# GpSimd's first level of the sums over negated scores: two heads in one instruction

## The reference, cut to what matters

```python
h = relu(layernorm(x))
q, k, v = h @ Wq.T, h @ Wk.T, h @ Wv.T + bv          # split into 12 heads
scores = q @ k.T * 384 ** -0.5 + bias                # 256 x 256 for each head; bias is 2 adj, then adj
row_nonzero = any(scores != 0, axis=-1)
p = softmax(where(row_nonzero, scores, -inf))        # nan becomes 0
x = x + (p @ v) @ Wo.T + bo
```

## Time and profile before

| what | value |
|---|---|
| median of 3 runs | 1733.27 us (1732.4 to 1737.6) |
| profiled execution, its own time | 1735.73 us |
| span of the profile | 1733.9 us |
| granted TensorE clock, mean | 0.994 |
| PE busy | 1661.9 us (96%) |
| DVE busy | 1545.5 us (89%) |
| ACT busy | 1356.5 us (78%) |
| POOL busy | 1360.2 us (78%), 1801 instructions |

### The profile page before, as it was taken

The page is one execution under the profiler, slowest core; times in us unless marked ns, Lnnn a source line. Parts: engine busy times, 40 slices in busy tenths (PEclk is TensorE's granted clock), DMA queues, the critical chain, the costliest instruction groups (busy, mean ns, idle before and its releaser), DMA issues.

```text
span 1733.9 us, 46852 instructions
## 1 busy us (share of the span) xinstructions
PE 1661.9 (96%) x14208; PEld 1496.1 (86%) x14208; DVE 1545.5 (89%) x5126; ACT 1356.5 (78%) x4233; POOL 1360.2 (78%) x1801
## 2 busy tenths in 40 slices
PE   6999999999999999999999999999999999999997
PEld 5888888888988888888889889888888888898885
DVE  6999999988989989889899899899999998998985
ACT  5878788788777787877887877787878878778775
POOL 4788787887877887878878878878778788788785
PEclk9999999999999999999999999999999999999998
DMA  7535535546446455355464464453553544544532
GB/s 228 122 85 127 121 95 137 112 100 141 101 111 139 91 123 125 94 134 113 99 141 105 107 141 94 118 131 93 130 121 93 138 109 104 141 94 118 132 72 67
DMA packets 92089, 201.50 MB, mean 116 GB/s; under 512 B 14528, under 2 KB 50880, under 8 KB 91840
## 3 DMA queue, kind: packets, MB, share of 16 engines
q1 hardware_dynamic: 91840, 198.50, 48.8%
HBM read 34.87 MB, written 12.58 MB: 27 GB/s over the span
## 4 chain that ended last, share of the span: by engine, by line
PE 93%; DVE 4%; issue 1%; POOL 1%; DMA 0%; ACT 0%; DVEq 0%; SPq 0%; POOLq 0%; ACTq 0%
PE misc_bank L735 23%; PE probT_bank L690 19%; PE misc_bank L775 13%; PE score_bank L672 11%; PE misc_bank L754 11%; PE values_bank L707 11%; PE values_bank L763 3%; PE misc_bank L715 2%; DVE values L532 2%; DVE normed L509 2%; ACT prob L410 0%; DMA stack<-split_qk 0%; DMA rows<-x 0%; DVE neg L548 0%; POOL quarter L336 0%
## 5 line engine op out<-in xcount | busy, mean ns | idle before, releaser
L410 ACT ACTIVATE prob<-neg,neg_max 128x256 f32<-128x256 f32 x1536 | 764.5, 501 | 124.9 <-DVE neg_max L548 110.5
L548 DVE CUSTOM_DVE_ANT_0 neg<-score_bank,bias 128x256 f32<-128x256 f32 x1536 | 577.7, 419 | 138.8 <-PE score_bank L672 124.5
L331 POOL TENSOR_TENSOR half<-neg 128x256 f32<-128x256 f32 x768 | 552.1, 737 | 163.1 <-DVE neg_max L548 162.8
L690 PE MATMUL probT_bank<-identity,prob 128*128 128x128 f32 x3072 | 430.6, 272 | 3.6 <-ACT prob L410 1.8
L421 ACT ACTIVATE probT<-probT_bank 128x512 f32<-128x512 f32 x640 | 368.2, 586 | 54.7 <-PE probT_bank L690 36.1
L690 PEld LDWEIGHTS probT_bank<-identity,prob 128*128 128x128 f32 x3072 | 353.2, 141 | 7.4 <-ACT prob L410 4.1
L672 PE MATMUL score_bank<-stack 96*128 96x256 f32 x1536 | 344.1, 313 | 2.6 <-DMA stack<-split_qk 2.1
L410 ACT ACTIVATION_READ_ACCUMULATOR prob<-neg,neg_max 128x1 f32 x1536 | 290.7, 189 | 0.0
L336 POOL TENSOR_TENSOR quarter<-half 128x512 f32<-128x512 f32 x192 | 248.0, 1292 | 15.1
L672 PEld LDWEIGHTS score_bank<-stack 96*128 96x128 f32 x1536 | 233.1, 191 | 29.2 <-issue 26.2
L707 PE MATMUL values_bank<-probT,values 128*32 128x256 f32 x3072 | 205.6, 385 | 1.1 <-ACT probT L421 1.1
(11 more groups left out here) (93 smaller groups left out, 3961.7 us busy)
## 6 DMA issues: line engine op xcount, KB each, us to landing
stack<-split_qk SPq DMA_DIRECT2D x768, 192.0 KB, 4.1
bias<-adj SPq DMA_DIRECT2D x64, 256.0 KB, 4.0
rows<-x SPq DMA_DIRECT2D x30, 384.0 KB, 4.5
out<-rows SPq DMA_DIRECT2D x30, 384.0 KB, 4.7
own_rows<-x SPq DMA_DIRECT2D x2, 384.0 KB, 4.7
out<-own_rows SPq DMA_DIRECT2D x2, 384.0 KB, 3.6
neg<-w0q SPq DMA_DIRECT2D x1, 576.0 KB, 4.4
prob<-w0k SPq DMA_DIRECT2D x1, 576.0 KB, 5.6
```

Of the source, the lines that this page charges most:

```text
L331: nc.gpsimd.tensor_tensor(half[:, step % GROUP, :, :], n[:, :, 0:N // 2], n[:, :, N // 2:N], ALU.add).then_inc(half_done, 1)
L410: nc.scalar.activation(prob[:, step % PROB, q, :], neg[:, step % NEG, q, :], ACT.Exp, scale=-1.0, bias=neg_max[u.k % 2][:, step, q:q + 1], ...
L548: nc.vector.tensor_tensor_reduce(out=neg[:, step % NEG, q, :], in0=score_bank[step % 2][:, q * N:(q + 1) * N], in1=bias[u.k % 4][:, q, :], ...
L690: mm = nc.tensor.transpose(probT_bank[step % 2][:, k * N + q * P:k * N + (q + 1) * P], prob[:, step % PROB, q, k * P:(k + 1) * P], identit ...
```

## The change

`add_half` takes two heads: it waits until both are negated, adds the halves of both in one instruction, and counts two. GpSimd's list is written anew for the pairs: six `add_half` for a unit in place of twelve. The half of head 0 no longer stands at the end of the slot before, but goes with head 1 at the start of its unit's own slot; `split_heads` of group 0 follows the first pair; `add_output_bias` stands ahead of the pair of heads 8 and 9. Nothing on the other engines is changed, their waits included.

```diff
@@ -326,10 +326,10 @@
             def add_half(u, step):
 
-                pool.wait_ge(neg_done, u.count(2 * HEADS, 2 * step + 2))
-                n = neg[:, step % NEG, :, :]
-                nc.gpsimd.tensor_tensor(half[:, step % GROUP, :, :], n[:, :, 0:N // 2], n[:, :, N // 2:N], ALU.add
-                                        ).then_inc(half_done, 1)
+                pool.wait_ge(neg_done, u.count(2 * HEADS, 2 * step + 4))
+                n = neg[:, step % NEG:step % NEG + 2, :, :].rearrange("p a q k -> p (a q) k")
+                h = half[:, step % GROUP:step % GROUP + 2, :, :].rearrange("p a q k -> p (a q) k")
+                nc.gpsimd.tensor_tensor(h, n[:, :, 0:N // 2], n[:, :, N // 2:N], ALU.add).then_inc(half_done, 2)
 
@@ -378,12 +378,11 @@
             def slot(attend, project, output, norm):
                 for stage, u, i in (
-                    (add_half, attend, 1), (add_half, attend, 2), (split_heads, output, 0), (add_half, attend, 3),
+                    (add_half, attend, 0), (split_heads, output, 0), (add_half, attend, 2),
                     (add_rest, attend, 0), (split_heads, output, 1), (split_heads, output, 2),
-                    (add_half, attend, 4), (add_half, attend, 5), (add_half, attend, 6), (add_half, attend, 7),
-                    (add_rest, attend, 1), (add_half, attend, 8), (add_output_bias, project, 0),
-                    (add_half, attend, 9), (invert_deviation, norm, 0), (add_half, attend, 10),
-                    (add_half, attend, 11), (add_rest, attend, 2), (add_half, project, 0),
+                    (add_half, attend, 4), (add_half, attend, 6),
+                    (add_rest, attend, 1), (add_output_bias, project, 0), (add_half, attend, 8),
+                    (invert_deviation, norm, 0), (add_half, attend, 10), (add_rest, attend, 2),
                 ):
```

## The result

The changed kernel takes 1777.38 us (median of 4 runs, 1775.57 to 1778.02), the kernel before beside it 1732.84 us: a ratio of 1.025, 95% interval 1.023 to 1.027. It is slower, as forecast, by 44.5 us where 25 were forecast; the time lies in the range. Between the two profiled executions the difference is 1775.57 - 1735.73 = 39.8 us.

The account below looks back on a forecast made before the run. A slot loop of PE and VectorE legs, with VectorE stretched by GpSimd's port use, was taken as the bound; 0.40 us over 61 slots plus 0.6 gave +25 us, median 1758, range 1734 to 1788.

Parts of the forecast that it names:

- What bounds the kernel: Each slot loops through PE (transposes to head 8's scores) and VectorE (head 8 to second value bias): 26.46 us.
- what the saved GpSimd work is worth: 73 us less work on GpSimd, worth nothing on the path because GpSimd has idle time.
- The price of a pair: One two-head `add_half` on GpSimd takes 1.28 us, like `quarter`; two single halves take 1.47.
- the spacing rule: Time GpSimd by start-to-start spacing: `quarter` at most 1.39 us; used for a pair, 40 us more, 1798.
- The end of the slot: Pair of heads 10 and 11 waits for head 11, delaying `quarter` and the normalisations: 0.43 us a slot.
- The sum: 0.40 us a slot over 61 slots, 24.4, plus 0.6 for the program's ends: +25 us, median 1758.
- The first half of the slot and group 1: From the first pair to `shares` of group 1: head 8 0 to 0.1 us late, group 0's `shares` 0.05.
- the slower turn: At `nonzero` of group 1, some slots before already had the delay: about 0.03 us a slot taken off.
- The range: The forecast time lies between 1734 and 1788 us, with about 0.80 of the chance.
- The bounds: Up to six pair prices a slot: 0.03 less each gives -11 us, 0.05 more each +18 us.
- two halves in disguise: GpSimd's pair takes the time of two halves, 1.47 us, giving 1825 us; chance 0.07.
- The first rival: At the slot's end the second normalisation gets the port before `quarter`, 1.08 us earlier: 1694 us; chance 0.11.

Follow-up runs that it names:

- the run with this pair alone: The kernel before with only heads 10 and 11 joined into one pair instruction, all other halves single: 1760.70 us, ratio 1.015.
- the first kernel with the added wait: The changed kernel, with GpSimd waiting for both normalisations after the pair of heads 10 and 11, before `quarter` of group 2: 1716.19 us, ratio 0.989.
- the kernel before with the added wait: The kernel before, with GpSimd waiting until both normalisations are done ahead of `quarter` of group 2: 1679.62 us, ratio 0.968.

## Why the prediction was right, and where its size was off

*What bounds the kernel* was right: two legs, PE and VectorE, and the loss on VectorE's. So was what the saved GpSimd work is worth: nothing.

*The price of a pair*, 1.28, measured 1.285. In the prediction the spacing rule of the Trainium skill (Perfetto Trace Analysis, "GPSIMD Engine Instruction") was applied across a semaphore and gave 1.39. This trace has two pairs in a row, and their starts, 907.32 and 908.58, are 1.26 apart, so that rule and the printed span nearly agree; across a semaphore it is 1.36 (919.13 to 920.49). And the VectorE instruction that stood behind the pair at 914.23 ended by its printed span: `nonzero` at 914.51 + 1.03 = 915.54, 0.02 after 914.23 + 1.29. Of the 73 us of work that GpSimd was to be spared, the line of the halves shows 60.7 (552.1 - 491.4), since busy time counts the overlap of two halves in a row once, and `eighth` takes 4.8 more. The second of the two pairs in a row, in a narrower window of GpSimd's timeline:

```profile
908.58 1.29 POOL L332 TENSOR_TENSOR half<-neg 128x512 f32<-128x512 f32 x1
```

*The end of the slot* was right in mechanism and near in size. The sum had 0.33 us there (0.43 less the 0.10 from earlier in the slot); the run with this pair alone shows 0.39, the two normalisations taking 2.62 in place of 2.23, and that is the 24.5 us between the profiled executions. The difference of 0.06 is the hop: I had 0.09 us from the negation to the pair, taken from single halves, and it was 0.15, since an increment of two puts the wait into an instruction of its own. That is a cost of the diff that I did not read out of it; undone in all pairs it is worth 8.5 us.

*The first half of the slot and group 1* is the other mis-sized term. I had head 8 at most 0.1 us late and head 11 0.10 late; head 8 was 0.15 late and head 11 0.22. Count from the value bias that opens the slot. These lines are of the kernel before, and then of the changed one, the last of them GpSimd's:

```profile
874.43 0.54 DVE L532 TENSOR_TENSOR values<-misc_bank,v_bias 128x384 f32<-128x384 f32 x1
...
877.76 0.42 DVE L548 CUSTOM_DVE_ANT_0 neg<-score_bank,bias 128x256 f32<-128x256 f32 x1
```
```profile
894.81 0.54 DVE L531 TENSOR_TENSOR values<-misc_bank,v_bias 128x384 f32<-128x384 f32 x1
...
898.13 0.42 DVE L547 CUSTOM_DVE_ANT_0 neg<-score_bank,bias 128x256 f32<-128x256 f32 x1
...
898.70 1.28 POOL L332 TENSOR_TENSOR half<-neg 128x512 f32<-128x512 f32 x1 [3.23 <-DVE neg_max L547]
```

The first pair starts 3.89 us into its slot, where the halves started after 3.83: it is the same hop again, 0.15 after head 1 in place of 0.08, and the prediction had none there. So the pair of heads 4 and 5 came 0.25 late (907.32 - 894.81 against 886.69 - 874.43), not 0.17, and its release took 0.28 us to reach VectorE (908.61 to 908.89) where I had allowed 0.2. `quarter` of group 1 came 0.02 earlier in its slot than before, not 0.11, and `shares` behind it ended 0.15 late, not 0.05 (911.72 - 894.81 against 891.19 - 874.43). Head 8's own delay is swallowed: `nonzero` ended 0.03 after `quarter` (911.27, 911.24) and had been held for about a microsecond. The run with heads 4 to 7 single does not test this, since there `nonzero` goes first.

*The sum.* To the 0.43 us of the forecast come 0.06 for the hop at the last pair and 0.12 for head 11's further delay, 0.61. 0.62 was measured, 38 us in the slots where 24 were forecast. The 0.03 that I took off for slots with the slower turn is there, but something as large stands against it. Before the change `quarter` won against `nonzero` of group 0 in 16 of 64 slots, against 2 of 64 in the new order with single halves, and head 11 was 0.03 later for it on average; but in some slots, as in the earlier trace rows, the normalisations were short, and on average they took 0.03 less than in the common slot. The other 4.7 us, between the 39.8 of the profiled executions and the 44.5 of the medians, are spread: the profiled execution of before lies 2.9 above its median, that of after 1.8 below.

*The range* held with some luck. The bounds that the prediction works out, 0.03 less and 0.05 more for each pair, give 1747 to 1776, and 1777.4 lies just beyond them; the 1785 and 1788 have no row behind them, and neither the hop nor the late list of GpSimd has a bound in it. The price of a pair, which was to set the bounds, was right to 0.005 us.

*The rivals.* VectorE did not get ahead of `quarter` at the end of the slot (0.06 us too late, as the rows of before said), and the pair was no two halves in disguise. The first rival's case, pairs with both normalisations ahead of `quarter`, is the first kernel with the added wait: 1716 us, where the rival had 1694. The second normalisation came 0.96 us earlier (2.60 - 1.64), not 1.08, and the loss to be undone was 0.62, not 0.43.

What a shorter leg of VectorE gives back was sized too low. The prediction ends the gain where the 0.72 us of idle time on TensorE are used up, 44 us; the kernel before with the added wait gained 54 to 57. The step that failed is to take a printed idle time for the price of the wait. TensorE's timeline of before has:

```profile
900.30 0.49 PE L715 MATMUL misc_bank<-identity,normed 128*128 128x128 f32 x3
901.51 0.55 PE L715 MATMUL misc_bank<-identity,normed 128*128 128x128 f32 x3 [0.72 <-DVE values L532]
901.99 0.42 PE L707 MATMUL values_bank<-probT,values 128*32 128x256 f32 x4
```

From the first transpose to the start of the next stage it is 901.99 - 900.30 = 1.69 us; with the wait gone it is 847.47 - 846.72 = 0.75. That is 0.94 us a slot, 57 us in 61: without the wait each matmul starts before the one ahead of it has ended by its printed time, and the wait costs that overlap too. None of this bears on the forecast, which had the leg longer and not shorter.

*What stays open.* With heads 10 and 11 single, 15 us of the loss are left. Making 8 and 9 single takes off 3.7, making 4 to 7 single then 25, which is 13.5 more than was left to lose. Alone, the latter took off nothing (1779.35). The parts don't add, since each shift changes who takes the port first. What does add up is where head 11 stands in the slot and how long the normalisations take. The table has means over the same 58 slots of each trace, in us, against the kernel before; head 11 is counted from the value bias that opens the slot.

| kernel | head 11 later by | normalisations longer by | slot longer by |
|---|---|---|---|
| changed | 0.20 | 0.41 | 0.61 |
| the last pair alone | -0.03 | 0.42 | 0.39 |
| 10 and 11 single | 0.21 | 0.00 | 0.21 |
| 4 to 7 single | 0.26 | 0.41 | 0.67 |
| 4 to 11 single | -0.26 | 0.01 | -0.25 |

So the 15 us that stay with heads 10 and 11 single are the late head 11. Which of the meetings in group 0 and group 1 makes it late by how much was not taken apart further, and for heads 8 and 9 there is only a time.

## What to carry to other kernels

A longer instruction saves its overhead and loses its seam: if it waits for two inputs where the first alone could be worked on, it starts late, and whatever shares its port stands behind all of it. So look first at what the two engines share, then at which of them has slack, and let the one with slack wait: one semaphore wait on GpSimd, which had time, was worth 3.2% here, while 55 us less work on GpSimd were worth nothing (1682.13 us with the pairs, 1679.62 without, the wait in both). And where a wait matters, try its semaphore in steps of one: here the steps of two cost 8.5 us.

## What the runs showed of the hardware that was not expected

- An increment of two on a GpSimd instruction moves its wait into an instruction of its own, 0.06 us more from release to start (0.15 against 0.09). 384 pairs have it; it counts where a pair waits for VectorE, at the first and the last of a slot, and is worth 8.5 us.
- VectorE gets the port at the seam of two back-to-back GpSimd instructions that overlap by 0.04 us in the trace, although the second has started by its printed time (both halves took 1.63 us in place of 1.43). The earlier trace rows has the same for a normalisation, and the prediction had read it so; the run adds that `shares` gets in the same way. The Trainium skill (SBUF — State Buffer, "SBUF: two separate sides") has the lock held for a whole instruction, and that holds here too, `shares` standing behind all 1.28 us of a pair; the printed start of a GpSimd instruction just isn't the moment at which it takes the port (the second half is printed from 862.14, while `shares` still got in at the end of the first).
- GpSimd's `quarter` 0.27 us later in its slot (medians over 58 slots, 15.44 against 15.17), for the second group of heads, makes the whole kernel 13.7 us faster (1719.96 against 1733.63, single halves in both from head 4 on): `nonzero` and `shares` both pass ahead of it.
- Whether `nonzero` or `quarter` goes first in group 0 hardly matters in itself: `nonzero` and `shares` together take 0.17 + 1.41 us before the change and 1.17 + 0.42 after it. It matters only when `shares` gets in front as well (0.18 + 0.43).
